# Order of the dense layer beside the wavelets: sums of the first chunk emptied ahead of the gate's weights, the attention's exponential ahead of the second root

## The reference

```python
xn = layernorm(x)                      # layer 0
s  = wavelet_block(xn)                 # 2 levels: filters h, g of 4 taps, every second position
     #   low = linear attention with 16 heads: q = elu(h) + 1, num / den
     #   2 levels back with the synthesis filters, then layernorm(xn + low)
g  = w3( gelu(h2( gelu(h1( silu(w1 xn) * (w2 xn) )) )) )
x  = x + s * silu(g)
xn = layernorm(x)                      # layer 1
ssm = xn + state_space(layernorm(xn))  # 16 states, a scan over positions
s  = W2 gelu(W1 layernorm(ssm) + b1) + b2 + ssm         # "dense layer", 1024 hidden
g  = mixture_of_experts(bf16(xn))      # rms norm, 8 logits, best 2, softmax, 8 experts
x  = x + s * silu(g)
```

## Time and profile before

| | |
|---|---|
| median of 3 runs | 2094.82 us |
| profiled execution, its own time | 2100.36 us |
| its span | 2098.6 us |
| PE busy | 1525.8 us (73%) |
| DVE busy | 1497.6 us (71%) |
| ACT busy | 1087.0 us (52%) |
| POOL busy | 899.2 us (43%) |
| stage 2 of the three full batches | from 541.4, 1022.4 and 1507.1 us |
| stage 2 of the last batch | from 1921.8 us |

### The profile page before, as it was taken

One profiled execution on the slowest core, in us unless ns is written; L12 is line 12 of the kernel. 1 busy time (PEld: TensorE's weight loads), 2 busy tenths in 40 slices (PEclk: granted clock), 3 DMA queues, 4 the chain that ended last, 5 costly groups with the idle time before them and its releaser, 6 DMA issues.

```text
span 2098.6 us, 16360 instructions
## 1 busy us (share of the span) xinstructions
PE 1525.8 (73%) x5296; PEld 645.4 (31%) x5296; DVE 1497.6 (71%) x1796; ACT 1087.0 (52%) x1475; POOL 899.2 (43%) x578
## 2 busy tenths in 40 slices
PE   4979658868868758868968677877878664335885
PEld 1434213423433223333433222333433221002321
DVE  2525158879758868878858887888838898996285
ACT  3434447667525657757434556767443544332343
POOL 3221214554205864453403784454501775343087
PEclk9989779989989989989989888998998986556998
DMA  7000100000100010000100000000100000001000
GB/s 170 1 0 11 51 0 1 0 20 1 60 10 0 31 40 1 1 21 0 61 10 0 30 21 21 1 20 1 60 11 0 10 21 20 8 12 60 0 0 21
DMA packets 12599, 42.42 MB, mean 20 GB/s; under 512 B 1866, under 2 KB 1890, under 8 KB 10466
## 3 DMA queue, kind: packets, MB, share of 16 engines
q1 hardware_dynamic: 11698, 35.08, 4.6%
q0 software_dynamic: 816, 6.30, 1.4%
HBM read 38.23 MB, written 4.19 MB: 20 GB/s over the span
## 4 chain that ended last, share of the span: by engine, by line
PE 37%; DVE 21%; issue 15%; ACT 15%; POOL 11%; SPq 0%; DMA 0%; POOLq 0%; DVEq 0%; ACTq 0%
PE psf L1190 6%; PE psf L1181 6%; PE psu L1351 5%; PE psy L1339 5%; POOL ap L656 3%; DVE st L1853 3%; ACT da L887 3%; POOL gate L651 3%; PE psf L1110 3%; DVE psu L1838 2%; PE psf L1160 2%; POOL gx L633 2%; PE psy L1160 2%; PE psu L1428 2%; ACT L887 2%
## 5 line engine op out<-in xcount | busy, mean ns | idle before, releaser
L633 POOL TENSOR_TENSOR gx<-gx,sy 128x1024 f32<-128x1024 f32 x120 | 303.5, 2529 | 229.7 <-DVE sy L1864 229.7
L651 POOL TENSOR_TENSOR gate<-gate,lin 128x512 f32<-128x512 f32 x128 | 172.1, 1345 | 472.1 <-DVE lin L1968 471.2
L1428 PE MATMUL psu<-ap,mw 128*128 128x512 f16 x512 | 148.3, 419 | 89.6 <-POOL ap L656 89.2
L887 ACT ACTIVATE da<-delta,aneg 128x512 f32<-128x512 f32 x256 | 164.2, 710 | 82.2 <-DVE st L1853 49.3
L624 POOL TENSOR_TENSOR g2p<-tf,g2p 128x512 fp32r<-128x512 f32 x64 | 87.2, 1368 | 229.8 <-ACT g2p L808 229.6
L1838 DVE TENSOR_TENSOR psu<-so,psu 128x1024 f32<-128x1024 f32 x128 | 156.6, 1224 | 36.2 <-PE psu L1301 35.7
L1190 PE MATMUL psf<-g1p,h2w 128*128 128x512 f16 x768 | 178.4, 380 | 4.9 <-ACT tf L785 4.9
L1190 PE MATMUL psf<-hp,h1w 128*128 128x512 f16 x768 | 175.4, 379 | 5.3 <-ACT tf L777 5.3
L959 ACT ACTIVATE gate<-gate 128x512 f32<-128x512 f32 x128 | 80.4, 628 | 182.5 <-DVE gate L1957 182.4
L1351 PE MATMUL psu<-hff,wf 128*128 128x512 f32 x256 | 128.2, 628 | 45.6 <-DVE so L1889 41.5
L1864 DVE TENSOR_TENSOR sy<-st,psu 128x1024 f32<-128x1024 f32 x128 | 156.1, 1220 | 6.5 <-DVE st L1853 2.6
(11 more groups left out here) (298 smaller groups left out, 3107.3 us busy)
## 6 DMA issues: line engine op xcount, KB each, us to landing
mw<-in_mlp_w SPq DMA_DIRECT2D x4, 2048.0 KB, 8.1
wf<-in_wf SPq DMA_DIRECT2D x5, 1024.0 KB, 4.8
xn<-in_x SPq DMA_DIRECT2D x8, 512.0 KB, 5.9
xr<-in_x SPq DMA_DIRECT2D x8, 512.0 KB, 3.6
x<-gx SPq DMA_DIRECT2D x8, 512.0 KB, 3.8
mw<-in_mlp_w SPq DMA_DIRECT2D x4, 1024.0 KB, 10.2
out<-outc SPq DMA_DIRECT2D x8, 512.0 KB, 3.1
h1w<-in_h POOLq DMA_DIRECT2D x1, 2048.0 KB, 12.5
```

The source lines that it names most:

```text
L633: pool.tensor_tensor(out, chunk(gx, c), sy[:, n % 2], ALU.add).then_inc(y_acc.sem, 1)
L651: pool.tensor_tensor(gate[:, r % NG], gate[:, r % NG], lin[r % NL][:], ALU.mult)\
L887: last = act.activation(da[:, n % 4, t], delta[c][:, t], ACT.Exp, scale=aneg[:, t, n:n + 1])
L1428: last = pe.matmul(psb[:, h], mw2[:, e, t, h * P:(h + 1) * P], ap2[r % NA][:, part], start=False, stop=(q == NQ - 1 and part == 1))
```

## The change

On PE, `lf_average(b1, 1)` moves ahead of the loop, from behind `hidden1(1)`. On ACT, `lf_square(1)` comes after the Gelu of tile 0 instead of tile 1, and `q_expo` gets a place of its own, k = 4, ahead of `expert_root(1)`. On both, the other pieces move one step of k forward, except for `expert_turn(1)`, which stays at 12. On DVE, `q0` is issued ahead of `expert_norm(1)`, and `block_out(b1, 0)` ahead of `expert_weights` instead of ahead of the first synthesis.

```diff
-LF_MEAN_AT, LF_VAR_AT, RMS_AT, RMS1_AT, ATTN_AT, LOGITS_AT, NUM_AT, EXP_AT, TURN_AT, TURN1_AT = 1, 3, 4, 6, 7, 8, 9, 10, 11, 12
+LF_SQ_AT, LF_VAR_AT, RMS_AT, Q_AT, RMS1_AT, ATTN_AT, LOGITS_AT, NUM_AT, EXP_AT, TURN_AT, TURN1_AT = \
+    0, 2, 3, 4, 5, 6, 7, 8, 9, 10, 12
@@ ScalarE, batch
+                    if b0 is not None and k == Q_AT:
+                        q_expo(b0, wave)
                     if b0 is not None and k == ATTN_AT:
-                        q_expo(b0, wave)
                         turn_copy(b0, wave)
...
-                    if k == LF_MEAN_AT:
+                    if k == LF_SQ_AT:
                         lf_square(b1, 1, b0 is not None)
@@ TensorE, batch
                 if b1 is not None:
+                    lf_average(b1, 1, b0 is not None)
                     for k in range(NC * KF + 1):
...
-                        if k == LF_MEAN_AT:
-                            lf_average(b1, 1, b0 is not None)
@@ VectorE, wavelets_and_attention
                     expert_norm(b1, 0)
-                    expert_norm(b1, 1)
                 dve.wait_ge(q_exp.sem, q_exp.at(b, 1))
                 dve.scalar_tensor_tensor(w.q0[:], w.l2[:], 0.0, w.qe[:], ALU.max, ALU.add).then_inc(q_done.sem, 1)
+                if b1 is not None:
+                    expert_norm(b1, 1)
...
                 if b1 is not None:
+                    block_out(b1, 0)
                     expert_weights(b1)
...
-                if b1 is not None:
-                    block_out(b1, 0)
                 synthesis(w.low2, w.h2b, quarter, lambda t, odd: w.low1[:, t, 1 + odd:half + odd:2], None)
```

## The result

The changed kernel takes 2068.86 us as the median of four runs (2068.19 to 2076.92), the kernel before 2094.55 us (2094.13 to 2094.92). The ratio is 0.9886, with a 95% interval of 0.9862 to 0.9911. The forecast was 2072.4 us with a range of 2063 to 2083. The interval leaves out 1, so the change is faster, by 25.7 us (1.1%) where 22.4 were forecast.

A forecast was written before the change was run, and what follows sets the result against it. Stage 2 was taken as one chain passing between engines, PE and DVE ending it almost together. Three full stages of -7.7 us (-23.1) and +0.7 in the last batch gave -22.4: 2094.8 to 2072.4 us, range 2063 to 2083.

The forecast's parts named there:

- 1 variance starts: Average moved into PE's gap ahead of the loop; PE's variance starts 3.4 us earlier than 559.23.
- 3 `q0` ends: Attention's exponential at k = 4 on ACT; `q0` is done at 571.8 us instead of 583.5.
- 4 second norm starts: After ACT's second root, DVE's second norm starts at 577.1 us instead of 578.85.
- 8 second turn: PE stands at `expert_turn(1)` for the first `cs` copy, some 5.6 us, until 615.7.
- step 5: Transposes and `attention_kv` on PE: start at 580.3 us instead of 585.90, at 1.2 GHz as before.
- the 3.4 us of the variance: Full batches, PE: with the average ahead of the loop, the variance starts 3.4 us earlier.
- step 7: On DVE, `block_out` ahead of `expert_weights` ends at 599.8 us; weights end at 602.8 instead of 607.95.
- The last batch: Stage without wavelets: 2.0 us delay from half clock behind the average, 1.3 gained; sum +0.7, bounds -2.6 to +3.4.
- half clock at the variance: Rival: new gaps ahead of the variance and at `expert_turn(1)` cost half clock; stage -4.6 us, total 2083; chance 0.15.
- `block_out` held DVE up: Rival: DVE's wait for the eighth down product delays the weights; 1.8 us slower a stage, 2103.6 us; chance 0.04.
- the rival with full clock: Rival: PE at full clock at `attention_kv` and `expert_turn(1)`, DVE last; -11.4 us a stage, 2060; chance 0.09.
- the stage ends no earlier: Rival: something of stage 3, such as a weight load, is late anyway; about 2094 us; chance 0.04.

The follow-up runs named there:

- e4: Changed kernel with the attention's exponential (`q_expo` at k = 6) and `q0` back at their old places: 2079.68 us, ratio 0.9944 to the kernel before.
- e5: Changed kernel with `lf_average(b1, 1)` back behind `hidden1(1)` on PE: 2068.13 us, ratio 0.9885 to the kernel before.
- e1: Kernel before with only `block_out(b1, 0)` moved ahead of `expert_weights` on DVE: 2086.44 us, ratio 0.9946 to the kernel before.
- e2: Changed kernel with `block_out(b1, 0)` back ahead of the first synthesis: 2076.31 us, ratio 0.9898 to the kernel before.
- e0: Changed kernel itself, run again as the base of its group: 2066.89 us, ratio 0.986 to the kernel before.
- e7: e6 with the logits ahead of `attention_kv` on PE, and the numerator and the gate's exponential at step 7: 2029.42 us, ratio 0.9699 to the kernel before.
- e8: e7 with the average back behind `hidden1(1)` in the last batch only: 2022.96 us, ratio 0.9671 to the kernel before.
- e3: Changed kernel with the second `expert_turn` at 14 instead of 12: 2060.08 us, ratio 0.9821 to the kernel before.
- e6: Changed kernel with the gate's exponential at loop position 8 and `block_out` back ahead of the first synthesis: 2039.11 us, ratio 0.975 to the kernel before.
- e9: e7 run again unchanged, as the base for e8: 2030.99 us, ratio 0.9704 to the kernel before.

## Why the prediction was right

Each step, in microseconds from the start of the last state sum in the first full stage (541.91 in the numbers of the prediction, 540.09 in the trace after):

| step | forecast | measured |
|---|---|---|
| 1 variance starts | 13.9 | 13.9 |
| 3 `q0` ends | 29.9 | 29.8 |
| 4 second norm starts | 35.2 | 35.0 |
| 5 `attention_kv` starts | 38.4 | 38.1 |
| 6 `kvm` ends | 51.1 | 50.1 |
| 7 `block_out` ends | 57.9 | 57.0 |
| 7 weights end | 60.9 | 59.9 |
| 8 second turn | 73.8 | 73.0 |
| 8 stage ends | 91.6 | 90.6 |

The chain, its order and the wait that takes the place of the one removed (5.6 forecast, 5.72 measured) were right. What was mis-sized is half clock in step 5. I let `attention_kv` run at 1.2 GHz as before (2.04 us). It took 1.13 us, and only the group behind it was at half clock (3.37). The gap ahead of it is now 2.94 us; before, two of 3.95 and 1.27 us stood ahead of it, and e4, which has those two again, has the 2.05 us again too. That is the 1 us that every later row of the table carries. In the third full stage that group ran at full clock too (1.88), and the two groups behind the turn were 3.72 and 2.85 us long, where the first stage has 3.67 and 1.88. Three stages of -8.6 to -9.6 in place of -7.7 make 4 us of difference to the forecast; the medians show 3.3.

The moved average was rightly fitted into the gap, but I tied the 3.4 us of the variance to it together with the loop position. e5 shows that the position gives most of it.

`block_out` has the price that step 7 gave it: e1 and e2 show 2 us a stage, and e1 refutes the reading that the longest wait of the profile was its cost. That reading would have forecast up to 11.6 us a stage.

The last batch came out at +0.6 (+0.7 forecast), from a delay of 1.4 us (2.0 taken) at the variance, less 0.8 us from `block_out` to the end (1.3 taken). But the delay does not come from the place that I gave. I looked for half clock in the two groups behind the average, since I read the 6.27 us for the same eight matmuls before as half clock; they were so only in part, for at full clock the eight take 3.60 us. The half clock is in the average itself, ahead of which PE now stands 6.69 us, since the two groups that filled that time are behind it:

```profile
1890.68 3.40 PE L1112 MATMUL psf<-so,meanw 128*128 128x512 f32 x4 [6.69 <-POOL so L634]
1893.91 3.60 PE L1341 MATMUL psy<-nrm,wf 128*128 128x512 f32 x8
```

In e0 the same code took 77.2 us there, 3.0 more than before, with 3.78 us for the average and 4.44 for the eight matmuls behind it. That lies within the stated bounds, but the single number was luck.

The rivals: half clock at the variance did not come; the 3.18 us gap ahead of it is followed by a group of 1.98 us. Behind the turn's gap of 5.72 us it came (3.67), in one group and not in two, except in the third full stage. `block_out` held DVE up by 0.8 us only (the gate's exponential is there at 596.19, the weights begin at 597.03), because the attention's chain came earlier by what was forecast. In the rival with full clock two numbers are off: half clock at `attention_kv` is 0.9 us in itself and 1.7 in the group behind it, not 1.7 in all; and its own sum has PE last (629.8) and not DVE (628.6). That the stage ends no earlier is refuted by the stages' lengths.

The rule of the Trainium skill that idle gaps between bursts of matmuls bring half rate ("TensorE: Matmul & The Clock Gate", HAM oscillation) agrees with the trace behind the turn; the shorter gap ahead of the variance did not bring it. The Trainium skill's figure for a table's drain ("ScalarE: Activation LUTs", What ACT_TABLE_LOAD costs) does not show in this trace either: ACT's Exp at 568.53 follows the load at 567.23 by 1.30 us, and the load begins 0.01 us behind the Gelu.

```profile
566.53 0.69 ACT L934 ACTIVATE hff<-psy,pk 128x512 f32<-128x512 f32 x1
567.23 1.28 ACT L822 ACT_TABLE_LOAD   x1
568.53 0.63 ACT L822 ACTIVATE qe<-qe 128x512 f32<-128x512 f32 x1
```

## What to carry to other kernels

The longest wait of an engine tells where it stands, not what it costs: follow what its releaser itself waited for, and price the wait that comes next when this one goes. In a chain over several engines, look for a piece whose data are complete while another piece, which waits, is ahead of it in the queue; here moving the logits ahead of `attention_kv`, with the numerator and the gate's exponential, took another 10.1 us from a stage (e7), more than the change itself. A loop position that is right with another row's work beside it can be wrong in the last pass without it: the early average cost 5.2 us there (e8).

## What the runs showed of the hardware that I had not expected

The same gap of 2.94 us ahead of `attention_kv` was followed by a group at 1.2 GHz in two full stages of one trace (3.37 and 3.42 us) and at 2.4 GHz in the third (1.88 us). The third is also the one whose average ran at half clock (3.40 us), some 36 us earlier. The traces of after, e0, e2, e3 and e6 have the same order on PE up to there, fifteen full stages in all. In nine the average took 1.98 us, and the group behind `attention_kv` 3.37 to 3.45 us. In the other six the average took 3.40 or 3.43 us, and that group 1.88 us. There is no exception. Why the two go together is not shown.

Runs of one kernel lie up to 9 us apart (e7: 2023.1 to 2032.3 us) with the same instructions. The dense stages are not where they part: the profiled runs of e7 and e9, one kernel, differ by 8.2 us in their spans (2021.3 and 2029.5), and their four dense stages agree to 0.1 us. The difference lies in the opening (2.0) and in the stretches between the stages (2.9, 0.6 and 2.8). PE's granted clock on average over the span was 0.884 in the faster of these two and 0.878 in the other. In e3 it was 0.878 to 0.883 in three runs and 0.875 in the slowest one. So a change that moves gaps of about 3 us around is not priced to better than one group (1.7 us) a gap, and single runs not to better than several microseconds.
